# Expert tiles ordered by the chunk they begin in, sixteen token tiles summed inside the expert loop, SiLU and kept copies on ScalarE, weight copies two pairs ahead

## What is computed

```python
x = layernorm(x + attention(x, Wq, Wk, Wv, Wfc))       # 16 heads of 16; softmax over the heads of one token
scores = sigmoid(x @ router_weight.T)                  # 32 experts, 4 groups, best 2 groups, best 4 experts
w = 2.5 * picked_scores / picked_scores.sum()
expert_e = (silu(x @ gate_w[e].T) * (x @ up_w[e].T)) @ down_w[e].T
shared   = (silu(x @ shared_gate_w.T) * (x @ shared_up_w.T)) @ shared_down_w.T
x = layernorm(x + sum_k w_k * expert_{e_k} + shared)
```

## Time and profile before

| | us |
|---|---|
| median of 3 runs | 746.73 (743.53 to 751.09) |
| span of the profiled execution | 591.0 |
| median less that span | 155.7 |
| PE busy in the span | 557.3 |
| DVE / ACT / POOL busy in the span | 372.0 / 278.8 / 289.8 |

### The profile page before, as it was taken

How to read it: one execution, slowest core, us unless ns; L and a number is a source line. 1 busy time by engine, 2 the same in 40 slices (tenths; PEclk the granted TensorE clock), 3 DMA queues, 4 the chain that set the end, 5 groups by cost and what they waited for, 6 DMA issues and landing times.

```text
span 591.0 us, 16304 instructions
## 1 busy us (share of the span) xinstructions
PE 557.3 (94%) x4916; PEld 437.1 (74%) x4917; DVE 372.0 (63%) x1250; ACT 278.8 (47%) x561; POOL 289.8 (49%) x301
## 2 busy tenths in 40 slices
PE   5989999999989999999969999999999999999985
PEld 2446578677665766675529999999999999887863
DVE  2032657698885887679544666666666665634774
ACT  2334453765837575253213555555555554530234
POOL 5000000654777765667741666666666665660221
PEclk9999999999999999999987999999999999999998
DMA  7999978987899799799423555555555554528996
GB/s 260 249 237 230 236 220 201 277 271 193 267 248 287 224 322 391 268 395 343 171 93 96 168 165 164 162 172 163 160 167 168 180 171 153 172 91 353 414 413 246
DMA packets 125820, 135.34 MB, mean 229 GB/s; under 512 B 76872, under 2 KB 107087, under 8 KB 125136
## 3 DMA queue, kind: packets, MB, share of 16 engines
q1 hardware_dynamic: 108288, 95.92, 54.3%
q0 software_dynamic: 12672, 34.10, 15.2%
q10 hardware_dynamic: 4816, 4.74, 2.3%
HBM read 74.79 MB, written 60.96 MB: 230 GB/s over the span
## 4 chain that ended last, share of the span: by engine, by line
PE 63%; DMA 15%; SPq 6%; issue 5%; POOL 4%; DVE 3%; ACT 2%; ACTq 0%; POOLq 0%; DVEq 0%
PE bank L933 54%; PE bank L1292 5%; DMA wgu_sb<-pick_rows 4%; DMA o_slots<-wgu_sb 4%; DMA wd_sb<-o_slots 3%; POOL expert_rows L534 3%; PE bank L1350 2%; DMA expert_rows<-stage,pos 2%; SPq L319 1%; SPq L328 1%; SPq L299 1%; PE bank L1348 1%; PE bank L981 1%; DMA q_slots<-wd_sb 1%; SPq L285 1%
## 5 line engine op out<-in xcount | busy, mean ns | idle before, releaser
L568 POOL DMA_INDIRECT pick_rows<-prod,ids x134 | 131.2, 979 | 93.9 <-ACT prod L885 46.2
L534 POOL DMA_INDIRECT expert_rows<-stage,pos x128 | 129.1, 1008 | 57.0 <-issue 34.8
L933 PE MATMUL bank<-prod 128*128 128x128 f32 x1088 | 135.0, 278 | 1.0 <-issue 1.0
L933 PEld LDWEIGHTS bank<-prod 128*128 128x128 f32 x1088 | 128.9, 195 | 1.7 <-issue 1.6
L933 PE MATMUL bank<-wd_sb,wqkv_sb 128*128 128x512 f32 x192 | 91.5, 614 | 6.5 <-DMA wqkv_sb<-in_wqkv 5.9
L1754 DVE COPY prod<-wgu_sb 128x512 f32 x136 | 54.1, 440 | 54.5 <-issue 51.8
L885 ACT ACTIVATE prod<-bank,kept 128x256 f32<-128x256 f32 x136 | 57.0, 470 | 37.7 <-PE bank L933 35.1
L933 PEld LDWEIGHTS bank<-wgu_sb 128*32 128x32 f32 x2048 | 58.6, 136 | 16.8 <-issue 13.6
L933 PE MATMUL bank<-wd_sb,prod 128*128 x272 | 70.1, 380 | 0.8 <-DVE prod L1785 0.8
L933 PE MATMUL bank<-wgu_sb 128*32 128x64 f32 x2048 | 65.8, 296 | 2.2 <-DMA wgu_sb<-k_slots 2.2
L933 PEld LDWEIGHTS bank<-wd_sb,wqkv_sb 128*128 128x128 f32 x192 | 35.1, 194 | 41.6 <-issue 35.8
(11 more groups left out here) (148 smaller groups left out, 774.6 us busy)
## 6 DMA issues: line engine op xcount, KB each, us to landing
prod<-expert_rows SPq DMA_DIRECT2D x136, 132.0 KB
wgu_sb<-pick_rows SPq DMA_DIRECT2D x32, 512.0 KB, 14.7
wgu_sb<-in_wgu SPq DMA_DIRECT2D x2, 2560.0 KB, 13.4
expert_rows<-pad_rows SPq DMA_DIRECT2D x4, 1056.0 KB, 19.0
wd_sb<-in_xT SPq DMA_DIRECT2D x8, 512.0 KB, 4.8
q_slots<-wd_sb SPq DMA_DIRECT2D x16, 256.0 KB
k_slots<-wd_sb SPq DMA_DIRECT2D x16, 256.0 KB
wgu_sb<-q_slots SPq DMA_DIRECT2D x16, 256.0 KB
```

Source lines behind the costliest of these rows:

```text
L534: pool.indirect_dma_start(xs, bass.IndirectOffsetOnAxis(ap=pos[e % 2][:, i, k:k + 1], axis=0), stage[:, i, k, :], None, bounds_check=XROWS ...
L568: pool.indirect_dma_start(z, bass.IndirectOffsetOnAxis(ap=index[:, j:j + 1], axis=0), rows[:, j, :], None, bounds_check=TOPK * NTOK - 1, o ...
L933: return pe.matmul(dst, lhsT, rhs, start=(k == 0), stop=(k == n - 1))
```

## The change

Six things are changed together.

- The table of tiles is ordered by class and then by expert, where class c (0 to 3) holds the tiles that begin with a row of chunk c, class 4 those of chunk 4, and class 5 the rest. It is worked out in 22 steps (`BSTEPS`) on 6 x 32 columns, from the counts kept after each of the first five chunks (`cums`). The number of tiles is the same.
- The last 17 groups run in a loop of their own. In each of 16 of them ACT issues the read of one token tile of chunks 0 to 3 (512 KB), and DVE adds its halves, and in the next group the quarters and `sx`.
- Chunk 4 is read when 4 groups are left to scatter, after SP's last row load; chunks 5 to 7 after the last scatter. Their zt buffers are all apart.
- ACT does Silu where it did Tanh; DVE's gate instruction is dropped and the weight in `idw` is no longer halved. One ACTIVATE of Silu stands after the last Tanh.
- ACT does `keep_meta`, at the head of its body; `label_rows` waits for it.
- DVE copies weights for pair n+2 at the end of the body of pair n, once its gate and up are done.

The tail takes the moments of chunks 0 to 3 from `sx` in SBUF, normalises in place in `sx`, and goes through the chunks in order. The core of the diff, without the table's steps and the declarations:

```diff
+FIRST_CHUNKS = 4
+FIRST_TILES = FIRST_CHUNKS * TPC
+CLASSES = FIRST_CHUNKS + 2
+VE = CLASSES * NE
...
+SUM_BANKS = {4: 6, 5: 0, 6: 2, 7: 4}
...
+SUM_LAG = 3
+SUM_GROUPS = FIRST_TILES
+SUM_START = SUM_GROUPS + 1
...
+        early_z = wsgu_sb.rearrange("p k c -> p (k c)")
+        early_sum = wqkv_sb.rearrange("p k c -> p (k c)")[:, 2 * CT:2 * CT + 2 * DM]
+        zt = {g: over(wgu_sb, (g - 5) * TPC * TOPK * DM, TPC * TOPK, DM).rearrange("p (t k) c -> p t k c", k=TOPK)
+              for g in range(FIRST_CHUNKS + 1, CH)}
+        zt[FIRST_CHUNKS] = over(stage.rearrange("p t k r -> p (t k r)"), 0, TPC * TOPK, DM)\
+            .rearrange("p (t k) c -> p t k c", k=TOPK)
...
+            def load_picks(g):
+                for t in range(TPC):
+                    at = (g * TPC + t) * P
+                    sp.dma_start(zt[g][:, t, :, :], z.rearrange("(n k) c -> n k c", k=TOPK)[at:at + P, :, :])\
+                        .then_inc(z_loaded[g][t], 16)
+            for par in range(2):
+                sp.wait_ge(y_scattered[par], quads * 32 - 32 * LATE_GROUPS)
+            load_picks(FIRST_CHUNKS)
             for par in range(2):
                 sp.wait_ge(y_scattered[par], quads * 32)
-
-            for g in range(CH):
-                if g >= ZWAYS:
-                    sp.wait_ge(S["d_ps"], TPC * (g - ZWAYS + 1))
-                for t in range(TPC):
-                    at = (LAST_ORDER[g] * TPC + t) * P
-                    sp.dma_start(zt[g % ZWAYS][:, t, :, :],
-                                 z.rearrange("(n k) c -> n k c", k=TOPK)[at:at + P, :, :])\
-                        .then_inc(z_loaded[g % ZWAYS][t], 16)
+            for g in range(FIRST_CHUNKS + 1, CH):
+                load_picks(g)
...
-        def quads_with_ends(eng, quads, body):
+        def quads_with_ends(eng, quads, body, beside=None):
             body(0, 0, False, True)
             body(0, 1, True, True)
-            with eng.Fori(1, quads - 1) as quad:
+            with eng.Fori(1, quads - (SUM_START if beside else 1)) as quad:
                 body(quad, 0, True, True)
                 body(quad, 1, True, True)
+            if beside:
+                with eng.Fori(0, SUM_GROUPS) as tile:
+                    quad = eng.snap(eng.to_reg(quads - SUM_START + tile))
+                    body(quad, 0, True, True)
+                    beside(quad, tile, 0)
+                    body(quad, 1, True, True)
+                    beside(quad, tile, 1)
...
+            act.activation(silu_first[:, :], neg_half[:, 0:1], ACT.Silu)
...
+            def keep_meta(n, par):
+                act.wait_ge(S["cmeta"], n + 1)
+                if not (isinstance(n, int) and n < 2):
+                    act.wait_ge(S["ids_ready"], n - 1)
+                    act.wait_ge(S["cy_copied"], n - 1)
+                act.activation(kept[par][:, :, :], meta[par][:, :, :], ACT.Copy).then_inc(S["kept"], 1)
             def pairs(quad, par, has_prev, has_next):
                 n = quad * 2 + par
+                keep_meta(n, par)
                 if has_next:
                     copy_xT(n + 1, 1 - par)
                 act.wait_ge(S["cgu_ps"], n + 1)
-                act.activation(cth[par][:, :], banks[par][:, 0:2 * P], ACT.Tanh, scale=0.5)\
+                act.activation(cth[par][:, :], banks[par][:, 0:2 * P], ACT.Silu)\
                     .then_inc(S["cth_ready"], 1)
                 if has_prev:
 
                     first = isinstance(n, int) and n < 3
                     copy_y(n - 1, 1 - par, None if first else (quad * 32 if par else quad * 32 - 32))
 
+            def load_early(quad, tile, par):
+                if par:
+                    return
+                act.wait_ge(S["e_free"], tile + 1)
+                for i in range(2):
+                    act.wait_ge(y_scattered[i], quad * 32 - 32 * SUM_LAG)
+                act.dma_start(early_z[:, :], z.rearrange("(n k) c -> n (k c)", k=TOPK)[bass.ds(tile * P, P), :])\
+                    .then_inc(S["e_z"], 16)
...
+            sum_down(5)
+            pe.wait_ge(S["cy_copied"], quads * 2)
+            sum_rows(4)
+            sum_down(6)
+            sum_down(7)
+            sum_rows(5)
+            sum_rows(6)
+            sum_rows(7)
...
+                if e < CLASSES - 1:
+                    dve.tensor_copy(cums[:, e, :], ranks_sb[:, TPC, :])
...
             def copy_meta(n, par, quad):
-
                 dve.wait_ge(xt_loaded[par], quad * 32 + 32)
                 if not (isinstance(n, int) and n < 2):
                     dve.wait_ge(S["kept"], n - 1)
                 dve.tensor_copy(meta[par][:, :, :], xt[par][:, :, ID:ID + 2]).then_inc(S["cmeta"], 1)
 
-            def copy_weights(n, par, quad, slot):
+            def find_weights(quad, slot):
                 word = quad_experts(dve, quad)
-                if not (isinstance(n, int) and n < 2):
-                    dve.wait_ge(S["cgu_ps"], n - 1)
+                return [dve.snap(dve.to_reg(expert(word, slot + j) * (KC * 2 * EI)), min_val=0,
+                                 max_val=(NE - 1) * KC * 2 * EI) for j in range(2)]
+            def copy_weights(par, found):
                 for j in range(2):
-                    last = dve.tensor_copy(ws[par][:, j, :],
-                                           wgu_sb[:, bass.ds(expert(word, slot + j) * (KC * 2 * EI), KC * 2 * EI)])
+                    last = dve.tensor_copy(ws[par][:, j, :], wgu_sb[:, bass.ds(found[j], KC * 2 * EI)])
                 last.then_inc(S["ws_ready"], 1)
 
             def label_rows(n, par, old, final=False):
+                dve.wait_ge(S["kept"], n + 1)
                 if old is not None:
                     dve.wait_ge(y_scattered[par], old)
                 to = ids_last if final else ids[par]
                 dve.tensor_copy(to[:, :], kept[par][:, :, 0]).then_inc(S["ids_ready"], 1)
 
-            def keep_meta(n, par):
-                dve.wait_ge(S["cmeta"], n + 1)
-                if not (isinstance(n, int) and n < 2):
-                    dve.wait_ge(S["ids_ready"], n - 1)
-                    dve.wait_ge(S["cy_copied"], n - 1)
-                dve.tensor_copy(kept[par][:, :, :], meta[par][:, :, :]).then_inc(S["kept"], 1)
-
-            def pairs(quad, par, has_prev, has_next):
+            def pairs(quad, par, has_prev, has_next, more=True, beside=None):
                 n = quad * 2 + par
-                if has_prev:
-                    keep_meta(n - 1, 1 - par)
                 if has_next:
                     copy_meta(n + 1, 1 - par, quad + par)
-                    copy_weights(n + 1, 1 - par, quad + par, 0 if par else 2)
                 dve.wait_ge(S["cth_ready"], n + 1)
-                dve.scalar_tensor_tensor(out=cth[par][:, :], in0=cth[par][:, :], scalar=1.0,
-                                         in1=banks[par][:, 0:2 * P], op0=ALU.add, op1=ALU.mult)\
-                    .then_inc(S["cgth_ready"], 1)
-                dve.wait_ge(S["cgth_ready"], n + 1)
                 if not (isinstance(n, int) and n < 2):
                     dve.wait_ge(S["cy_ps"], n - 1)
                 dve.tensor_tensor(hT[par][:, :], cth[par][:, :], banks[par][:, 2 * P:4 * P], ALU.mult)\
                     .then_inc(S["ch_ready"], 1)
                 if has_prev:
-                    dve.wait_ge(S["kept"], n)
                     first = isinstance(n, int) and n < 3
                     label_rows(n - 1, 1 - par, None if first else (quad * 32 if par else quad * 32 - 32))
-
+                if beside:
+                    beside()
+                if more:
+                    found = find_weights(quad + 1, 2 * par)
+                    dve.wait_ge(S["cgu_ps"], n + 1)
+                    copy_weights(par, found)
+            def sum_halves(tile):
+                dve.wait_ge(S["e_z"], tile * 16 + 16)
+                if not isinstance(tile, int):
+                    dve.wait_ge(S["e_sum"], tile)
+                dve.tensor_tensor(early_sum[:, :], early_z[:, 0:2 * DM], early_z[:, 2 * DM:], ALU.add)\
+                    .then_inc(S["e_free"], 1)
+            def sum_row(tile):
+                dve.wait_ge(S["e_free"], tile + 2)
+                dve.tensor_tensor(early_sum[:, 0:DM], early_sum[:, 0:DM], early_sum[:, DM:], ALU.add)\
+                    .then_inc(S["e_half"], 1)
+                dve.wait_ge(S["e_half"], tile + 1)
+                dve.tensor_tensor(sx[:, bass.ds(tile * DM, DM)], sx[:, bass.ds(tile * DM, DM)], early_sum[:, 0:DM],
+                                  ALU.add).then_inc(S["e_sum"], 1)
+            dve.memset(slot_first[:, :], 0.0).then_inc(S["e_free"], 1)
             copy_meta(0, 0, 0)
             dve.wait_ge(S["big_w"], 16 * NBIG)
-            copy_weights(0, 0, 0, 0)
-            quads_with_ends(dve, quads, pairs)
-            keep_meta(quads * 2 - 1, 1)
-            dve.wait_ge(S["kept"], quads * 2)
+            copy_weights(0, find_weights(0, 0))
+            copy_weights(1, find_weights(0, 2))
+            pairs(0, 0, False, True)
```

(39 more changed lines are left out.)

213 lines of the change are left out of this document (107 added, 106 removed).

## The result

The changed kernel takes 712.12 us (median of 4 runs, 707.32 to 716.42) where the kernel before takes 745.13 (742.82 to 751.09): a ratio of 0.955, interval 0.948 to 0.962.

A forecast was written before the change was run, and what follows sets the result against it. The prediction took PE to bound the expert loop, DMA and PE the tail; -25.5 + 3 + 2 + 1 = -19.5 us, so span 571.5 and time 746.7 - 19.5 = 727, range 717 to 741.

The forecast's parts named there:

- tail: After the last scatter: chunks 0 to 4 no longer read and added there, 25.5 us gained (bounds 20 to 29).
- early reads late on the weight copy: Last 17 groups: DVE's wait for the read makes weights 0.37 us late for gate/up, 3 us over 16 groups.
- scatters: Expert loop: early reads and chunk 4's burst delay scatters whose y_sb is reused after two pairs, 2 us (0 to 6).
- table and entries: Before the loop, 22 table steps for 14, 0.5 us; entering a second loop on DVE and ACT, 0.5 us.
- rebalancing: Expert loop: Silu, kept copies on ACT and earlier weight copies make the loop no faster, 0 us.
- 155.7 us lie around the span; nothing in the diff touches them and they are kept: Whole kernel: median time 746.7 against profiled span 591.0; the difference was kept unchanged in the forecast time.
- PE is busy throughout, so none of this makes the loop faster: 0: Expert loop: PE bound it at 3.09 us a pair, so gate and weight-copy changes were priced at 0.
- chain (a): Tail, DMA, one of three chains (DMA, DVE, PE): 8.9 MB of reads and stores, 21.7 us from 534 to 555.5.
- signs of being wrong: In the profile: second-half groups above 6.9 us, PE at half clock in the tail, or loop start later than 311.
- Rival 4: Expert loop: 16 reads cost 1.5 us each in stalls, 24 us back, about 745 us; chance 0.05.
- Rival 1: Expert loop: DVE and the early reads become the bound, gain only 6 us, time 741; chance 0.13.
- Rival 3: Expert loop: ACT loads tables twice a pair if Copy and Silu share none, time 829; chance 0.04.

The follow-up runs named there:

- e14: Changed kernel without its rebalancing (early tiles alone), on a second-kind chip, where the kernel before takes 731 to 747 us: 704.27 us, 0.962 of before.
- e13: Changed kernel with each early read issued as two of 256 KB, one a pair, sums one pair later, second-kind chip: 709.18 us, 0.955 of before.
- e10: Kernel before with the rebalancing alone (Silu and kept copies on ScalarE, weights two pairs ahead), first-kind chip (before 594 to 596 us): 594.28 us, 0.997 of before.
- e6: Kernel before with the rebalancing alone (Silu and kept copies on ScalarE, weights two pairs ahead), second-kind chip: 731.21 us, 0.979 of before.
- e16: Kernel before with two groups in one iteration of the expert loop, work otherwise unchanged, second-kind chip: 721.27 us, 0.968 of before.
- e2: Changed kernel, unchanged, on a first-kind chip: 595.56 us, 1.001 of the kernel before.
- e9: Changed kernel with its 16 early reads cut to 16 bytes a partition, sums kept, output incomplete, first-kind chip: 572.30 us, 0.963 of the kernel before.

## Why the forecast was right and wrong

| step of the forecast | us | first kind | second kind |
|---|---|---|---|
| tail | -25.5 | -25.6 (73.3 to 47.7) | -24.8, -26.1 (75.7 to 50.9, 49.6) |
| early reads late on the weight copy | +3 | VectorE waits 0.4 us, once | 5.9 us, 8 times (changed kernel) |
| scatters | +2 (0 to 6) | +22 (128.1 against 106.4) | +9 (142.1 against 132.7, across chips) |
| these two together, by the whole stretch against before | +5 | +25 (128.1 against 103.3) | -2 (e14), +2 (e13) |
| table and entries | +1 | -1 to +4 in the start of the loop (+3 in e10, with the old table) | -0.2, +4.4 on one chip |
| rebalancing | 0 | 0 (e10) | -15.5 alone |
| sum | -19.5 | +0.8 measured | -33 measured |

The step that failed first is the one ahead of the sum: "155.7 us lie around the span; nothing in the diff touches them and they are kept". They lie inside the span of the executions that were timed. The profile's 591.0 and the times of 743 to 751 are of two kinds of chip, so a loop of 217 us bound by PE was no picture of the loop that was timed. From it follows the term that failed on that kind, where the time fell below the range: "PE is busy throughout, so none of this makes the loop faster: 0". There PE is idle for 22 us of each stretch (1.3 us a group), and the rebalancing alone is worth 15.5 us. The 13.5 us beyond the forecast are of that size. No chip of the second kind gave a trace of before and one of the changed kernel, so they can't be laid out stretch by stretch. What makes those chips slower is open.

*The tail* was right, in the changed kernel to within a microsecond: the kernels with early tiles need 46.9 to 51.0 us from pair 67 on (e6, e10 and e16 keep the old tail, 72.9 to 74.6), so the gain on the first kind is 22 to 26 by the version. What the forecast had less right is which chain ends it. It chose PE's; in e2 the last piece before the final adds is the DMA:

```profile
567.38 15.90 DMA wgu_sb<-pick_rows
583.30 0.69 DVE wgu_sb L1900
```

From the last scatter's landing (561.5) to the end of this piece (583.3) are 21.8 us, where the forecast's chain (a) had 21.7. It put all three chains within a microsecond, so that the wrong choice left the number as it was.

*Early reads.* The landing was sized right: 4.0 us taken, 3.9 to 4.8 and 4.0 in the median measured. The issue was earlier than taken, 1.3 us after gate/up (Silu starts 460.56, the issue stands at 461.90) and not 1.9. By the forecast's own sum the weights are then ready at 1.3 + 4.0 + 1.75 = 7.1, before the 7.28 of gate/up, and the groups, longer by the scatters, give them 1.5 us more. The loop stretch of e9 still takes 3 us more than before's (106.4 against 103.3); what takes them was not traced.

```profile
DMA to landing us min/median/max: 3.9/4.0/4.8
```

*Scatters* is the mechanism that was named and mis-sized: "meet at most one of four scatters a group; 0.6 of slack takes most of it". The read of the group shown meets at least two, issued 0.1 us before it and 1.3 after it, and the first lands 2.1 us late; the cycle of 5.6 us becomes 7.7 where 6.18 was free, 1.5 us a group in sixteen groups, and 22 were measured. The forecast's own signs of being wrong came true here: groups of the second half above 6.9 us (7.8), and a loop start later than 311 (312.4, in e2). The traffic was judged by its mean (a loop at 0.51 of the DMA's time), when the reads' bytes take a landing that the loop waits for from 2.6 us to 4.4 and more. In the DMA view of 455 to 462 us a read is 144 packets, nine on each of the 16 engines:

```profile
q10 hardware_dynamic: 144, 0.52, 25.8%
```

The Trainium skill ("DMA: Bandwidth & Descriptors", Queues, rings and completion order) says that an engine takes its queues in turn, but drains some 9 to 17 descriptors of one before it goes to the next. The forecast drew on the turns and left the second half out; by it an engine may carry its whole nine of a read in one turn. The trace agrees as far as the scatters go, which see no turn in 1.8 us while the read is there; row loads do get packets in between (12.5% beside 79.2%), which the rule in this reading does not explain.

*Rival 4*, the change buys nothing at 1.5 us of stalls a group, had a chance of 0.05. On the first kind it is what happens, 1.4 us a group, through the scatters and not through reads landing over 6 us. *Rival 1* falls: VectorE is not the bound. *Rival 3* falls: one ACT_TABLE_LOAD more than before, 1.28 us at the start of the loop, and Silu takes what Tanh took (0.38). The Trainium skill's rule ("ScalarE: Activation LUTs", Table sets) that cheap functions such as copy are in every set is borne out for Silu's: no load stands in the loop.

```profile
L913 ACT ACT_TABLE_LOAD x1 | 1.3, 1283 | 0.0
L947 ACT ACTIVATE prod<-bank x68: 378/383/385, 317.4 to 551.7; 128x256 f32<-128x256 f32 x68
```

What would have told it beforehand: the span and the time of one and the same execution side by side. In the profiles of all kernels here they are 1.7 to 2.2 us apart, so a gap of 155 us says that the profile is of another chip or execution, and every slack read from it needs a second value.

## What to carry to other kernels

Compare a profile's span with its own execution's time before costing anything; where they are far apart, the bound of each stage is not known, and the forecast needs a case for each. Work moved from a tail into a loop is not priced by the loop's mean DMA share but by how far its transfers delay the landing that the loop waits for: look for buffers that are reused after two steps and count their slack first. Two delays in one loop need not add (in e14 the group cost about the longer), so a change can be nearly free on one chip and cost its whole gain on another.
